# Expert probabilities turned in 32x32 blocks on VectorE and placed by DMA, with the attention product in the second slot

## The chip, the cores and the metric

The kernel runs on one core of a Trainium2 chip. The metric is the device time of one execution in microseconds. Beside the times stands one profiled execution of the same program; every row quoted below is from its trace. TensorE (PE) multiplies matrices and writes PSUM banks, VectorE (DVE), ScalarE (ACT) and GpSimd (POOL) work elementwise, SyncE (SP) issues the DMAs.

## What is computed

The input x is (8, 512, 256). It is normalized, and two branches are added to it: a causal attention with 16 heads of width 16, and a block whose attention is a mixture of experts, followed by two layer norms and a feed-forward net. Nearly all time goes into the expert attention and the causal one, which the kernel does together, a pair of heads of one batch at a time:

```python
def _gate(x, Wsel):
    s = jax.nn.sigmoid(jnp.einsum('bsd,hed->bhse', x, Wsel))
    _, idx = jax.lax.top_k(s, K)
    mask = jax.nn.one_hot(idx, E, dtype=s.dtype).sum(-2)
    return s * mask
...
q = _rope(jnp.einsum('bsd,hdp->bhsp', x, Wq))
k = _rope(jnp.einsum('bsd,hdp->bhsp', x, Wk))
gv = _gate(x, Wsel_v)
v = jnp.einsum('bsd,bhse,hedp->bhsp', x, gv, Wv)
att = jax.nn.softmax(jnp.einsum('bhsp,bhtp->bhst', q, k) / np.sqrt(P), axis=-1)
o = jnp.einsum('bhst,bhtp->bhsp', att, v)
go = _gate(x, Wsel_o)
return jnp.einsum('bhsp,bhse,hepd->bsd', o, go, Wo)
...
score = jnp.einsum('bhqd,bhkd->bhqk', Q, K) / jnp.sqrt(jnp.asarray(D_K, x.dtype))
```

## The kernel before

There are 64 pairs: 8 batches times 8 pairs of heads. A pair is worked off in a software pipeline over two passes of a loop body. The body of step `it` does the scores and probabilities of pair `it`; beside them it does the tail of the pair before (the jobs "behind") and the preparation of the next pair (the jobs "ahead"). Only the first pass and the last ones (FIRST, LAST, TAIL) leave jobs out; 62 passes (INNER) are alike, and a step below is one of them.

A step has 8 slots. Slot s begins with the scores of unit s+1 (the last with unit 0 of the next pair). Even units are the expert attention: for one block of 128 queries, 128x512 scores for each of the two heads. Odd units are the causal attention, 128 to 512 columns wide. Behind the scores of a unit, VectorE takes the negative row maxima (`row_max`, "the maxima", L1136), ScalarE the exponentials into `probs` (`exps`, L957), and then TensorE transposes the 128x128 blocks of `probs` into PSUM (`turn(s)`, L718; 8 of them for the two heads of an even unit, 2 to 8 for an odd one), and ScalarE copies them to `pt_e` (even) or `pt_c` (odd) (`turned`, L977). That is the key-by-query form that the attention product needs.

Between these, each engine fills its slot with jobs from a table written out by hand (PE_FILL, ACT_FILL, DVE_FILL, POOL_FILL). Each engine runs its own list strictly in order and waits on semaphores for the others. The jobs are:

- P 0 to 3 (PE, L673): projections of the next pair for a block of 128 rows; ScalarE copies the result to `raw`.
- CH 0 and CH 1 (DVE, L1181 to L1205): the two halves of the choice of the two best experts, from `raw`.
- V 0 to 7 (PE, L673): the values of all experts; VectorE multiplies with the gates and sums over the experts (L1157, L1159), the gate of V 0 after CH 1.
- QK 0, 1 (PE, L745), QH (ACT), QL (DVE): the queries and keys turned, in two parts of high and low order. RP, RS, RA, PC on GpSimd, PA, PB, SQ, SK on ScalarE, ST on PE and SO on ScalarE prepare rotation and the causal operands.
- AT (PE, L773): the attention product of the pair before, 16 matmuls of 512 columns from `pt_e` and `v_sb`. VC (POOL, L569) copies the next values to `v_sb` once AT is done.
- ON (DVE, L1232): AT's bank times `scale` to `oo`, which frees the bank. U e (DVE, L1239): `oo` times the output gate of expert e, to `uf`. UH e (ACT, L1041) and UL e (POOL, L573): high and low part of it.
- J e (PE, L799): six matmuls of `u_h`, `u_l` with the output weights of expert e, into two banks of sums. YA (DVE, L1245) adds the sums to `y_sb` at the end of the step.
- AC (PE, L785), its eviction (ACT) and VA: the causal product.

P, V, QK, AT and AC take two PSUM banks in turn, in the order of PE_FILL, and wait until the bank's last content has been taken. In both tables V 0 takes the bank that AT had, so it waits for ON.

SP's list in a step is: two stores of the causal output, two loads of `go` (the output gates, spread over the partitions), a load of `xx` when V 3 is done, four small stores of the reciprocal sums, two loads of them as `scale`, a load of `xx` when V 7 is done, two loads of `go`, four stores of the gates. Once in 8 steps it also loads new weights.

## Time and profile before

| | us |
|---|---|
| median of 3 runs | 3404.29 |
| lowest and highest | 3403.39 and 3406.31 |
| span of the profiled execution | 3401.4 |
| PE busy in it | 3233.1 (95%) |
| DVE busy | 2439.7 (72%) |
| ACT busy | 1961.5 (58%) |
| POOL busy | 1441.9 (42%) |
| DMA, share of 16 engines | 32.9% |

The profiled execution's own time is its span; the median is 2.9 us above it. How to read it: busy time is the sum over instructions; matmuls overlap at their ends, so the distance from one start to the next is the better measure of what a group costs. Rows of the view in order of time merge equal neighbours ("x8"), so the time of such a row covers all of them. "[4.37 <-ACT raw]" means that the engine had been idle for 4.37 us and what ended that. The span has a head of about 112 us before the loop, the loop, and a feed-forward tail from about 3110 us on.

### The profile page before, as it was taken

How to read it: one execution, taken by the hardware profiler on the slowest of the kernel's cores; microseconds unless marked ns; L12 is line 12 of the kernel's file. 1: busy time of each engine (PE TensorE's matmuls, PEld its weight loads, DVE VectorE, ACT ScalarE, POOL GpSimd, SP SyncE). 2: the span in 40 equal slices, each digit the busy share in tenths (PEclk: the TensorE clock that was granted, in tenths of full speed). 3: DMA queues.
4: the chain of work that ended last, by engine and by line, in shares of the span. 5: the costliest groups of instructions: out<-in, count | busy, mean ns of one | idle time of the engine just before them, and what ended most of it. 6: DMA issues, size and time to landing. Idle time of an engine off the chain costs nothing.

```text
span 3401.4 us, 64468 instructions
## 1 busy us (share of the span) xinstructions
PE 3233.1 (95%) x18240; PEld 2378.9 (70%) x18240; DVE 2439.7 (72%) x4708; ACT 1961.5 (58%) x4509; POOL 1441.9 (42%) x1215
## 2 busy tenths in 40 slices
PE   1699999999999999999999999999999999997998
PEld 1577777777777777777777777777777777775765
DVE  6577777777777777777777777777777777775554
ACT  2466666656666666666666666666666666664121
POOL 4144355445443454345543554434534543442212
PEclk9999999999999999999999999999999999999999
DMA  5223333334233333233233332333332433333221
GB/s 165 76 71 87 95 90 85 77 76 109 76 84 87 84 98 81 75 100 96 69 87 76 96 98 77 76 104 81 84 87 68 114 81 75 84 75 110 72 83 62
DMA packets 115937, 295.18 MB, mean 87 GB/s; under 512 B 33856, under 2 KB 54592, under 8 KB 99264
## 3 DMA queue, kind: packets, MB, share of 16 engines
q1 hardware_dynamic: 115904, 294.78, 32.9%
q8 instruction: 15, 0.25, 0.0%
q14 instruction: 18, 0.15, 0.0%
HBM read 262.74 MB, written 31.98 MB: 87 GB/s over the span
## 4 chain that ended last, share of the span: by engine, by line
PE 85%; issue 6%; DVE 5%; ACT 3%; DMA 1%; POOL 0%; ACTq 0%; SPq 0%; DVEq 0%; POOLq 0%
PE bank L673 27%; PE bank L799 22%; PE bank L718 9%; PE bank L773 7%; PE bank L688 5%; PE bank L905 4%; PE bank L897 3%; PE bank L693 3%; PE bank L745 2%; PE bank L754 2%; ACT probs L957 2%; DVE uf L1239 1%; DVE oo L1232 1%; PE bank L694 1%; ACT pt_e L977 1%
## 5 line engine op out<-in xcount | busy, mean ns | idle before, releaser
L573 POOL TENSOR_TENSOR u_l<-uf,u_h 128x512 fp32r<-128x512 f32 x512 | 716.1, 1409 | 722.6 <-ACT u_h L1041 722.4
L1136 DVE TENSOR_REDUCE nmax<-bank 128x1 f32<-128x512 f32 (+3 forms) x1024 | 551.8, 579 | 305.0 <-PE bank L688 297.8
L673 PE MATMUL bank<-wv_h,xx 128*128 128x512 f32 x2048 | 755.0, 410 | 7.1 <-DVE vm L1157 7.1
L957 ACT ACTIVATE probs<-bank,nmax 128x512 f32<-128x512 f32 (+3 forms) x1024 | 590.7, 610 | 253.2 <-DVE nmax L1136 253.1
L1041 ACT ACTIVATE u_h<-uf 128x512 fp32r<-128x512 f32 x512 | 321.7, 632 | 696.9 <-DVE uf L1239 683.6
L673 PEld LDWEIGHTS bank<-wv_h,xx 128*128 128x128 f32 x2048 | 386.0, 188 | 155.8 <-issue 59.6
L718 PEld LDWEIGHTS bank<-ident_sb,probs 128*128 128x128 f32 x3328 | 388.3, 141 | 106.4 <-issue 51.3
L718 PE MATMUL bank<-ident_sb,probs 128*128 128x128 f32 x3328 | 451.3, 274 | 1.6 <-ACT stackT L1032 0.9
L569 POOL TENSOR_TENSOR v_sb<-v_next,zero_hb 128x512 f32<-128x512 f32 x64 | 74.2, 1160 | 891.9 <-PE bank L773 877.4
L799 PE MATMUL bank<-u_h,wo_h 128*128 128x512 f32 x1024 | 427.1, 417 | 5.0 <-ACT u_h L1041 3.2
L1239 DVE TENSOR_TENSOR uf<-oo,go 128x512 f32<-128x512 f32 x512 | 416.2, 823 | 8.8 <-POOL u_l L573 6.6
L799 PE MATMUL bank<-u_h,wo_l 128*128 128x512 f32 x1024 | 405.9, 396 | 0.0
L799 PE MATMUL bank<-u_l,wo_h 128*128 128x512 f32 x1024 | 405.0, 396 | 0.0
L673 PE MATMUL bank<-wv_l,xx 128*128 128x512 f32 x1024 | 404.8, 395 | 0.0
L1157 DVE TENSOR_TENSOR vm<-bank,gv 128x512 f32<-128x512 f32 x512 | 348.4, 681 | 41.6 <-PE bank L673 41.5
L1159 DVE TENSOR_REDUCE v_next<-vm 128x64 f32<-128x512 f32 x512 | 351.3, 686 | 17.6
L673 PE MATMUL bank<-wq_h,xx 128*128 128x384 f32 x1024 | 280.4, 344 | 12.8 <-DMA xx<-xs_d 12.7
L977 ACT ACTIVATE pt_e<-bank 128x512 f32<-128x512 f32 x512 | 276.1, 594 | 5.1 <-PE bank L718 0.5
L799 PEld LDWEIGHTS bank<-u_h,wo_h 128*128 128x128 f32 x1024 | 192.4, 188 | 66.5 <-issue 24.4
L773 PE MATMUL bank<-pt_e,v_sb 128*64 128x512 f32 x1024 | 233.8, 598 | 0.0
L1191 DVE TENSOR_SCALAR vm<-raw 128x128 f32<-128x128 f32 x64 | 14.5, 227 | 296.6 <-ACT raw L992 296.6
L799 PEld LDWEIGHTS bank<-u_h,wo_l 128*128 128x128 f32 x1024 | 192.5, 188 | 46.5
(141 smaller groups left out, 5164.2 us busy)
## 6 DMA issues: line engine op xcount, KB each, us to landing
go<-go_d SPq DMA_DIRECT2D x256, 512.0 KB, 6.5
xx<-xs_d SPq DMA_DIRECT2D x128, 512.0 KB, 3.5
oo<-scale_d SPq DMA_DIRECT2D x128, 128.0 KB, 2.9
a_d<-a_out SPq DMA_DIRECT2D x128, 128.0 KB, 2.3
pt_c<-in_x SPq DMA_DIRECT2D x16, 512.0 KB, 4.7
st<-in_wv SPq DMA_DIRECT2D x16, 512.0 KB, 5.8
st<-in_wo SPq DMA_DIRECT2D x16, 512.0 KB, 7.2
go_d<-go_turned SPq DMA_DIRECT2D x256, 8.0 KB
```

The lines of the kernel that those rows point to most:

```text
L573: nc.gpsimd.tensor_tensor(u_l[:, e % 2], uf[:, e % 2], u_h.bitcast(f32)[:, e % 2], ALU.subtract).then_inc(ul_done, 1)
L673: last = nc.tensor.matmul(out, lhs, rhs, start=n == 1, stop=n == 3 * len(chunks))
L718: mm = nc.tensor.transpose(o[:, c * NP:(c + 1) * NP], probs[:, s % 2, j, c * NP:(c + 1) * NP], ident_sb[:])
L773: mm = nc.tensor.matmul(o[j * P:(j + 1) * P, :], v_sb[:, k, j, :], pt_e[:, j, k, :], start=k == 0, stop=k == TT - 1)
L799: mm = nc.tensor.matmul(ybank[i][:], w[:, e, c], u[:, e % 2], start=e == 0 and k == 0, stop=e == E - 1 and k == 2, skip_group_check=True)
L957: nc.scalar.activation(probs[:, s % 2, j, 0:w], sbank[j][:, 0:w], ACT.Exp, bias=nmax[:, 2 * s + j:2 * s + j + 1], **kw).then_inc(exp_done, 1)
L977: nc.scalar.activation(dst[:, j, 0:m, qt * NP:(qt + 1) * NP], tbank[j][:, 0:m * NP].rearrange("q (c m) -> q c m", m=NP), ACT.Copy).then_in ...
L1041: nc.scalar.activation(u_h[:, i % 2], uf[:, i % 2], ACT.Copy).then_inc(uh_done, 1)
L1136: nc.vector.tensor_reduce(nmax[:, 2 * s + j:2 * s + j + 1], sbank[j][:, 0:w], AX.X, ALU.max, negate=True).then_inc(nmax_ready, 1)
L1157: nc.vector.tensor_tensor(m, o[:].rearrange("q (c e) -> q c e", e=E), g, ALU.mult).then_inc(free, 1)
L1159: nc.vector.tensor_reduce(v_next[:, t, j, :], m, AX.X, ALU.add).then_inc(v_ready, 1)
L1239: nc.vector.tensor_tensor(uf[:, i % 2], oo[:, 0], go[:, i], ALU.mult).then_inc(u_ready, 1)
```

## The change

The transposes of the even units leave TensorE. VectorE gets four jobs XT 0 to 3: one instruction each that transposes `probs` of an even unit in blocks of 32x32 to a new buffer `pt_b`, which holds two units. When two are there, SP issues 16 DMAs (`spread_blocks`) that carry the blocks to their places in `pt_e`, each for one of four groups of 32 source partitions and one of four of target partitions. ScalarE no longer evicts the even turns, and its exponentials of an even unit wait until the one before has been transposed. XT 2 waits until the first 16 DMAs have landed, XT 0 of the next step and AT until the second 16 have. The queries lie in `pt_e` in another order, which ON undoes.

AT moves from slot 0 to slot 1, with AC behind it, ON and U 0 move from slot 0 to slot 1 behind CH 1, and the tables are dealt anew. The weights of the projections are staged in the buffer of the value weights, and are split by GpSimd in the third slot and not the seventh, once in 8 steps. The zeros that GpSimd adds are now read from one column.

```diff
-PE_FILL = [[("P", 0), ("P", 1), ("P", 2), ("P", 3), ("AT", 0)],
-           [("AC", 0), ("V", 0)],
-           [("J", 0), ("V", 1), ("J", 1)],
-           [("V", 2), ("J", 2), ("J", 3)],
-           [("V", 3), ("J", 4), ("V", 4)],
-           [("QK", 0), ("J", 5), ("QK", 1)],
+PE_FILL = [[("P", 0), ("P", 1), ("P", 2), ("P", 3)],
+           [("AT", 0), ("AC", 0)],
+           [("V", 0), ("J", 0), ("V", 1)],
+           [("J", 1), ("V", 2), ("J", 2)],
+           [("V", 3), ("J", 3), ("V", 4)],
+           [("QK", 0), ("J", 4), ("QK", 1), ("J", 5)],
            [("V", 5), ("J", 6), ("V", 6)],
            [("V", 7), ("ST", 0), ("ST", 1), ("J", 7)]]
-ACT_FILL = [[("P", 0), ("P", 1), ("P", 2), ("P", 3), ("EX", 0), ("UH", 0), ("UH", 1)],
-            [("AC", 0), ("VA", 0), ("PA", 0)],
-            [("UH", 2), ("UH", 3), ("VN", 0)],
-            [("UH", 4), ("UH", 5)],
-            [("UH", 6), ("PB", 0)],
-            [("QH", 0), ("QH", 1), ("UH", 7)],
-            [("SQ", 0), ("SK", 0)],
+ACT_FILL = [[("P", 0), ("P", 1), ("P", 2), ("P", 3), ("EX", 0), ("PA", 0)],
+            [("AC", 0), ("VA", 0), ("UH", 0)],
+            [("UH", 1), ("VN", 0), ("UH", 2)],
+            [("UH", 3)],
+            [("UH", 4), ("PB", 0), ("UH", 5)],
+            [("QH", 0), ("QH", 1), ("UH", 6)],
+            [("SQ", 0), ("SK", 0), ("UH", 7)],
             [("SO", 0), ("SO", 1)]]
-DVE_FILL = [[("CH", 0), ("ON", 0), ("U", 0), ("U", 1)],
-            [("CH", 1)],
-            [("U", 2), ("V", 0), ("U", 3)],
-            [("V", 1), ("U", 4), ("V", 2), ("U", 5)],
-            [("V", 3), ("U", 6)],
-            [("V", 4), ("QL", 0), ("QL", 1), ("U", 7)],
-            [("V", 5), ("RECIP", 0)],
+DVE_FILL = [[("XT", 0), ("CH", 0)],
+            [("CH", 1), ("ON", 0), ("U", 0)],
+            [("XT", 1), ("U", 1), ("V", 0), ("U", 2), ("V", 1)],
+            [("U", 3), ("V", 2)],
+            [("XT", 2), ("U", 4), ("V", 3), ("U", 5), ("V", 4)],
+            [("QL", 0), ("QL", 1), ("U", 6)],
+            [("RECIP", 0), ("XT", 3), ("V", 5), ("U", 7)],
             [("V", 6), ("V", 7), ("YA", 0)]]
-POOL_FILL = [[("VC", 0)],
-             [("UL", 0), ("UL", 1)],
-             [("UL", 2), ("RP", 0), ("UL", 3)],
-             [("RP", 1), ("UL", 4), ("RS", 0)],
-             [("RA", 0), ("UL", 5)],
-             [("UL", 6), ("PC", 0)],
-             [("UL", 7)],
-             []]
+POOL_FILL = [[],
+             [("VC", 0)],
+             [("UL", 0), ("RP", 0), ("UL", 1)],
+             [("UL", 2), ("RP", 1), ("RS", 0)],
+             [("UL", 3), ("RA", 0), ("UL", 4)],
+             [("UL", 5), ("PC", 0)],
+             [("UL", 6)],
+             [("UL", 7)]]
...
+        pt_b = sb("pt_b", [NP, 2, 4 * TT, 2, 32])
+        wq_st = st[:, 0, 0:KC * NPROJ]
...
+            def spread_blocks(it, kind, half, blocks):
+                if blocks[0] == 0:
+                    sp.wait_ge(blocks_ready, it * TT + 2 * half + 2)
+                for i in blocks:
+                    a, c = i // 4, i % 4
+                    sp.dma_start(pt_e[c * 32:(c + 1) * 32].rearrange("q j k (a s) -> q (j k) a s", a=4)[:, :, a, half * 64:(half + 1) * 64],
+                                 pt_b[a * 32:(a + 1) * 32].rearrange("q j (k c) t m -> q (j k) c (t m)", c=4)[:, :, c, :]).then_inc(pt_in[half], 16)
             def body(p, b, kind, before=None, after=None, weights=False, more=False):
                 it = p * B + b
                 if weights:
-                    sp.wait_ge(wq_split, p + 1)
+                    sp.wait_ge(wo_split[0], p + 1)
                     load_wq(p + 1)
-                    for j in range(2):
-                        sp.wait_ge(wo_split[j], p + 1)
-                        load_wv(p + 1, j)
+                    sp.wait_ge(wo_split[1], p + 1)
+                    load_wv(p + 1, 1)
                 if before is not None:
                     store_a(*before, kind, it)
+                spread_blocks(it, kind, 0, range(16))
+                if before is not None:
                     sp.wait_ge(u_ready, it * E - E // 2)
                 load_go(it, 0)
                 if more:
                     for j in range(2):
                         sp.wait_ge(wv_split[j], p + 2)
                         load_wo(p + 1, j)
+                if weights:
+                    sp.wait_ge(wq_split, p + 2)
                 if after is not None:
                     v_full(kind, it, 3)
                     load_x(after[1], 0)
+                if weights:
+                    load_wv(p + 1, 0)
                 spread_rden(it)
+                spread_blocks(it, kind, 1, range(6))
                 load_scale(it)
                 if after is not None:
                     v_full(kind, it, 7)
                     load_x(after[1], 1)
+                spread_blocks(it, kind, 1, range(6, 16))
                 if before is not None:
                     sp.wait_ge(u_ready, it * E)
                 load_go(it, 1)
...
-                    if wv_next and s == SLOTS - 2:
+                    if wv_next and s == 2:
...
-                    turned_before(6)
+                    for half in range(2):
+                        pe.wait_ge(pt_in[half], 256 * of + 256)
...
+                if s % 2 == 0:
+                    act.wait_ge(blocks_ready, n * TT + qt)
...
+                    elif name == "XT":
+                        dve.wait_ge(exp_done, it * UNITS + 4 * i + 2)
+                        if i == 2:
+                            dve.wait_ge(pt_in[0], 256 * it + 256)
+                        elif i == 0 and kind != FIRST:
+                            dve.wait_ge(pt_in[1], 256 * it)
...
-                        nc.vector.tensor_tensor(oo[:, 0], o[:], scale, ALU.mult).then_inc(free, 1)
+                        turned_q = o[:].rearrange("q (a t m) -> q t a m", a=4, t=TT)
+                        nc.vector.tensor_tensor(oo[:, 0].rearrange("q (t a m) -> q t a m", a=4, t=TT), turned_q,
+                                                scale.rearrange("q (t a m) -> q t a m", a=4, t=TT), ALU.mult).then_inc(free, 1)
```

In VectorE's list, at the start of the loop (nmax is the maxima; vm, best, gv, go_turned the choice; oo is ON, uf is U). Before:

```order
L1136 TENSOR_REDUCE nmax<-bank 128x1
...
L1191 TENSOR_SCALAR vm<-raw 128x128
...
L1232 TENSOR_TENSOR oo<-bank,oo 128x512
L1239 TENSOR_TENSOR uf<-oo,go 128x512 x2
L1136 TENSOR_REDUCE nmax<-bank 128x1
...
L1181 TENSOR_REDUCE best<-vm 128x16
...
L1205 STREAM_TRANSPOSE go_turned<-go_rows 128x64
```

And after:

```order
L1161 TENSOR_REDUCE nmax<-bank 128x1
...
L1245 STREAM_TRANSPOSE pt_b<-probs 128x32x32
...
L1216 TENSOR_SCALAR vm<-raw 128x128
...
L1161 TENSOR_REDUCE nmax<-bank 128x1
...
L1230 STREAM_TRANSPOSE go_turned<-go_rows 128x64
...
L1265 TENSOR_TENSOR oo<-bank,oo 128x512
...
L1273 TENSOR_TENSOR uf<-oo,go 128x512
```

A transpose stands ahead of the choice, and ON with the first U has moved from between its halves to behind the second.

In TensorE's list, from the last projection of the next pair on, with the semaphores waited for (pt_e is AT, pt_c is AC, wv_h is V 0, the first u_h is J 0). Before:

```order
L673 MATMUL bank<-wq_h,xx 128x384
...
L773 MATMUL bank<-pt_e,v_sb 64x512 [waits t_free1,t_free0]
L773 MATMUL bank<-pt_e,v_sb 64x512 x7
...
L718 MATMUL bank<-ident_sb,probs 128x128 x3
...
L688 MATMUL bank<-k_h,q_h 128x512 [waits exp_done]
...
L785 MATMUL bank<-pt_c,va 32x512 [waits t_free0,t_free1,va_ready,w_free1]
...
L673 MATMUL bank<-wv_h,xx 128x512 [waits wv_split0,w_free0]
```

And after:

```order
L694 MATMUL bank<-wq_h,xx 128x384
L709 MATMUL bank<-k_h,q_h 128x512 [waits exp_done]
...
L795 MATMUL bank<-pt_e,v_sb 64x512 [waits pt_in1,pt_in0]
L795 MATMUL bank<-pt_e,v_sb 64x512 x7
...
L807 MATMUL bank<-pt_c,va 32x512 [waits t_free1,t_free0]
...
L714 MATMUL bank<-stackT 128x256 [waits exp_done]
...
L694 MATMUL bank<-wv_h,xx 128x512 [waits wv_split0,w_free0]
```

AT now stands behind the even scores, waits for the DMAs instead of ScalarE's evictions, and the turn between AT and those scores is gone.

SP's list after, from the stores of the causal output to the last load of `go`:

```order
L393 DMA a_d<-a_out 64x512
...
L416 DMA pt_e<-pt_b 32x8x64 [waits blocks_ready]
L416 DMA pt_e<-pt_b 32x8x64 x15
...
L386 DMA go<-go_d 64x2048
...
L373 DMA xx<-xs_d 128x1024
...
L402 DMA scale_d<-rden_t 8x32 x3
...
L416 DMA pt_e<-pt_b 32x8x64 x5
L408 DMA oo<-scale_d 64x512 [waits rden_stored]
...
L416 DMA pt_e<-pt_b 32x8x64 x10
```

The three groups of `pt_e<-pt_b`, 16, 6 and 10, are new; the rest stands in the order of before.

## Rows read from the trace of the kernel before

**Rows 1.** One stretch: busy us of PE, PEld, DVE, ACT, POOL; clock, DMA share, GB/s.

```profile
700.00:1166.00 466.00, 459.81 (x2680) 339.95 (x2679) 347.65 (x650) 293.55 (x680) 207.76 (x181) 1.00 0.35 88
```

**Rows 2.** In order of time, PE, one step: start, us, engine, line, what, count.

```profile
1519.66 0.23 PE L693 MATMUL bank<-stackT 96*128 96x128 bf16 x1
...
1524.40 3.65 PE L773 MATMUL bank<-pt_e,v_sb 128*64 128x512 f32 x16
...
1529.00 0.50 PE L688 MATMUL bank<-k_h,q_h 64*128 64x512 f32 x2
...
1529.90 1.28 PE L785 MATMUL bank<-pt_c,va 128*32 128x512 f32 x16
...
1533.90 0.49 PE L799 MATMUL bank<-u_h,wo_h 128*128 128x512 f32 x1
...
1549.65 1.04 PE L718 MATMUL bank<-ident_sb,probs 128*128 128x128 f32 x8
1550.62 0.50 PE L688 MATMUL bank<-k_h,q_h 64*128 64x512 f32 x2
...
1554.70 0.38 PE L693 MATMUL bank<-stackT 96*128 96x512 bf16 x1
...
1566.25 0.23 PE L693 MATMUL bank<-stackT 96*128 96x128 bf16 x1
```

**Rows 3.** In order of time, DVE, the same step.

```profile
1525.10 0.23 DVE L1191 TENSOR_SCALAR vm<-raw 128x128 f32<-128x128 f32 x1 [4.37 <-ACT raw L992]
...
1528.21 0.69 DVE L1232 TENSOR_TENSOR oo<-bank,oo 128x512 f32<-128x512 f32 x1 [0.58 <-PE bank L773]
...
1531.97 1.39 DVE L1182 TENSOR_TENSOR vm<-vm,best 128x128 f32<-128x128 f32 x1
1533.40 0.29 DVE L1183 TENSOR_TENSOR vm<-vm,rank_sb 128x128 f32<-128x128 f32 x1
...
1536.46 0.72 DVE L1136 TENSOR_REDUCE nmax<-bank 128x1 f32<-128x256 f32 x2
1537.11 0.67 DVE L1239 TENSOR_TENSOR uf<-oo,go 128x512 f32<-128x512 f32 x1
...
1538.41 0.69 DVE L1159 TENSOR_REDUCE v_next<-vm 128x64 f32<-128x512 f32 x1
...
1551.62 1.29 DVE L1136 TENSOR_REDUCE nmax<-bank 128x1 f32<-128x512 f32 x2 [2.38 <-PE bank L688]
...
1555.51 0.68 DVE L1239 TENSOR_TENSOR uf<-oo,go 128x512 f32<-128x512 f32 x1
```

**Rows 4.** In order of time, POOL, the same step.

```profile
1528.23 1.16 POOL L569 TENSOR_TENSOR v_sb<-v_next,zero_hb 128x512 f32<-128x512 f32 x1 [16.62 <-PE bank L773]
1530.68 2.53 POOL L573 TENSOR_TENSOR u_l<-uf,u_h 128x512 fp32r<-128x512 f32 x2 [1.29 <-ACT u_h L1041]
1538.52 1.28 POOL L573 TENSOR_TENSOR u_l<-uf,u_h 128x512 fp32r<-128x512 f32 x1 [5.30 <-ACT u_h L1041]
```

**Rows 5.** Transposes on DVE, by tile: count, duration ns least, median, most.

```profile
L1205 DVE STREAM_TRANSPOSE go_turned<-go_rows x64: 245/245/247, 111.8 to 3027.9; 128x64 f32<-128x64 f32 x64
...
L1228 DVE STREAM_TRANSPOSE rden_t<-rden x64: 211/211/214, 160.0 to 3084.0; 128x32 f32<-128x32 f32 x64
```

**Rows 6.** Issues on SP in order of time; last, the page's row of a landing.

```profile
29.01 0.50 SPq L358 DMA_DIRECT2D xs_d<-u_l  x1
...
1559.19 1.31 SPq L397 DMA_DIRECT2D scale_d<-rden_t  x4
...
1565.09 3.36 SPq L374 DMA_DIRECT2D go_d<-go_turned  x4
...
a_d<-a_out SPq DMA_DIRECT2D x128, 128.0 KB, 2.3
```

**Rows 7.** PE ahead of the loop: a wait, and the stretch behind it.

```profile
140.34 0.28 PE L693 MATMUL bank<-stackT 96*128 96x256 bf16 x1 [3.25 <-ACT probs L957]
...
141.60:145.00 3.40, 3.40 (x15) 2.72 (x15) 3.23 (x9) 1.19 (x4) 0.00 (x0) 0.60 0.00 0
```

More of the change, by code:

```diff
@@ L112, in t_jobs @@
                 out.append(j)
-        if kind in (FIRST, INNER, LAST):
+        if kind in (FIRST, INNER, LAST) and s % 2 == 1:
             out.append(("turn", s))
@@ L347, in _ @@
             load_wq(0)
-            for j in range(2):
-                load_wv(0, j)
+            load_wv(0, 1)
             for b in range(B):
@@ L359, in _ @@
                                      part_x[b % 2][k].bitcast(f32).rearrange("q (h c) -> q h c", h=2)).then_inc(xs_out[b % 2], 16)
+                if b == 0:
+                    sp.wait_ge(wq_split, 1)
+                    load_wv(0, 0)
                 if b == 1:
@@ L408, in body @@
                 if weights:
-                    sp.wait_ge(wq_split, p + 1)
+                    sp.wait_ge(wo_split[0], p + 1)
                     load_wq(p + 1)
-                    for j in range(2):
-                        sp.wait_ge(wo_split[j], p + 1)
-                        load_wv(p + 1, j)
+                    sp.wait_ge(wo_split[1], p + 1)
+                    load_wv(p + 1, 1)
                 if before is not None:
                     store_a(*before, kind, it)
+                spread_blocks(it, kind, 0, range(16))
+                if before is not None:
                     sp.wait_ge(u_ready, it * E - E // 2)
@@ L568, in do @@
                         pool.wait_ge(v_ready, it * 8 + 8)
-                        nc.gpsimd.tensor_tensor(v_sb[:].rearrange("q t j c -> q (t j c)"), v_next[:].rearrange("q t j c -> q (t j c)"), zero_hb[:], ALU.add).then_inc(vc_ready, 1)
+                        nc.gpsimd.tensor_tensor(v_sb[:].rearrange("q t j c -> q (t j c)"), v_next[:].rearrange("q t j c -> q (t j c)"), zero_hb[:].to_broadcast([NP, S]), ALU.add).then_inc(vc_ready, 1)
                     elif name == "UL":
@@ L716, in turn @@
                         pe.wait_ge(exp_done, it * UNITS + 2 * s + j + 1)
-                        for c in range(TT if s % 2 == 0 else s // 2 + 1):
-                            mm = nc.tensor.transpose(o[:, c * NP:(c + 1) * NP], probs[:, s % 2, j, c * NP:(c + 1) * NP], ident_sb[:])
+                        for c in range(s // 2 + 1):
+                            mm = nc.tensor.transpose(o[:, c * NP:(c + 1) * NP], probs[:, 1, j, c * NP:(c + 1) * NP], ident_sb[:])
                         mm.then_inc(t_full[j], 1)
@@ L756, in turn_stack, with causal_turned @@
                     mm.then_inc(t_full[i], 1)
-                def turned_before(s):
+                def causal_turned():
                     for i in range(2):
                         if kind == TAIL:
-                            pe.wait_ge(t_free[i], t_at(LAST, it, i, ("turn", s)) + 1)
+                            pe.wait_ge(t_free[i], t_at(LAST, it, i, ("turn", 7)) + 1)
                         else:
-                            pe.wait_ge(t_free[i], t_at(INNER, it, i, ("turn", s)) + 1 - NT[i])
+                            pe.wait_ge(t_free[i], t_at(INNER, it, i, ("turn", 7)) + 1 - NT[i])
                 def attend():
@@ L852, in body @@
                         do(job)
-                    turn(s)
+                    if s % 2 == 1:
+                        turn(s)
             body(PRO, 0)
@@ L1055, in body @@
                         do(job)
-                    turned(s)
+                    if s % 2 == 1:
+                        turned(s)
             body(PRO, 0)
@@ L1213, in do @@
                         choose(i)
+                    elif name == "XT":
[4 more added lines that the diff above has]
+                            dve.wait_ge(pt_in[1], 256 * it)
+                        nc.vector.transpose(pt_b[:, :, :, i % 2, :].rearrange("q j c m -> q (j c) m"), probs[:, 0].rearrange("q j s -> q (j s)")).then_inc(blocks_ready, 1)
                     elif name == "QL":
```

18 lines of the change are left out of this document (9 added, 9 removed).

## The prediction

> **What bounds the kernel now.** I read the busy shares by stretch first. In ten steady steps of 46.6 us each TensorE is busy for 459.8 of 466.0 us, VectorE for 347.7, ScalarE for 293.6, GpSimd for 207.8, and the DMA engines for 0.35 of the time [rows 1]. So TensorE is the bound, but no other engine is far enough away to be forgotten: VectorE has 11.8 us to spare in a step. Then I read one step in order of time, from 1519.66 to 1566.25, 46.59 us [rows 2]; times below are counted from its start. The reader is to see how tightly two loops close. TensorE projects the next pair (P 0 to 3, until 4.74), runs the attention product AT there, and starts J 0, the first output product, at 14.24. VectorE sat idle 4.37 us for the projections (CH 0 starts at 5.44), and J 0 is fed by ON, U 0, UH 0 and UL 0, which run on VectorE, ScalarE and GpSimd in turn [rows 3, 4]. In the kernel before, that feed starts at 8.55 (ON) and is ready just in time. The chain of releasers is therefore TensorE nearly everywhere, yet the slack of the feed is a fraction of a microsecond.
>
> **What is removed.** Four of eight turns of a step go, those of 8 transposes. One lasts from 1549.65 to 1550.62, 0.97 us [rows 2]; four are 3.88 us. TensorE alone would fall to 46.59 - 3.88 = 42.7 us a step. ScalarE loses the eight evictions to pt_e, which is worth nothing by itself, since it isn't the bound.
>
> **What is added on VectorE.** Four block transposes of 128x1024. Two sizes are in the trace: 211 ns for 32 columns, 245 ns for 64 [rows 5]. That is 1.06 ns a column, so 0.21 + 992 x 1.06 ns = 1.27 us each, 5.1 us a step; lower bound half of it (a wider output could do two columns at once), upper bound 2.0. VectorE goes to 34.8 + 5.1 = 39.9 us, under 42.7. The first of the four, XT 0, stands ahead of CH 0, in the idle time of 4.37 us, and costs nothing there as long as the DMA of the step before has landed by 5.44 - 1.27 = 4.2.
>
> **What is moved, and this is the main term.** AT goes from the first slot to the second, so that the DMA has time. With it go ON and U 0, and in VectorE's list they now stand behind CH 1, the second half of the choice. Work the feed of J 0 again, from the start of the step:
> CH 0 starts at 5.44 as before, since P 0 to 3 aren't moved, and ends at 7.97 (the idle time of 0.58 ahead of ON at 8.55 gives this end) [rows 3]. The maxima of scores 2 take 1.25, to 9.25. CH 1 has a first step of 0.3, then L1182, which lasted 1.39 us, and 3.06 us from L1183 to the next maxima [rows 3]. L1182 is a product of 128x128 that takes 0.3 us like its neighbours when GpSimd is idle; in the rows GpSimd ran two u_l from 1530.68 to 1533.21, and L1182 ended just behind them [rows 3, 4]. So such a VectorE operation waits for a GpSimd operation that is running. Without that wait CH 1 is 3.7 and ends at 12.95. But GpSimd's copy of v (VC, 1.16 us [rows 4]) now starts when AT has been issued, at 4.74 + 0.90 (scores 2) + 3.65 = 9.3 [rows 2], 0.1 ahead of L1182: L1182 then ends at 10.8 and CH 1 at 13.8. I take this value, and keep 12.95 as the other end. ON adds 0.7: 14.5. From the start of a U to the end of its u_l the trace shows 1537.11 to 1539.80, 2.69 us [rows 3, 4]: J 0 starts at 17.3 (16.4 without the wait of L1182).
> From J 0 on, the same work is left on TensorE as before (V 1 to 7, J 0 to 7, QK, ST, all scores): 46.59 - 14.24 = 32.35, less three of the removed turns, 29.4. The step is 17.3 + 29.4 = 46.7 us. So almost all that the transposes give back is waited away at two places, V 0 (its bank is freed by ON: TensorE arrives at 9.3 + 1.3 for AC + 0.6 for the small turn and scores 3 = 11.2, and waits until 14.5) and J 0.
>
> **A second wait, at J 6.** In slot 5 VectorE now does the gate of V 4 first, then the maxima of scores 6, QL 0 and 1, and U 6. From the maxima's start to the start of U the trace shows 1551.62 to 1555.51, 3.89 us; the gate with its reduction is about 0.63 + 0.69; U to u_l is 2.69 [rows 3, 4]. From the end of V 4 to J 6 that is 7.9 to 8.1 us. TensorE needs for it slot 5, 4.08 (1550.62 to 1554.70) and 1.4 for the J that is now there too, then scores 7 and V 5, 2.0: 7.5 [rows 2]. So 0.5 us more, bounds 0 and 1.0. I take 0.6: 47.3 us.
>
> **The DMAs.** 32 are added in a step, 16 behind XT 1 and 6 + 10 behind XT 3, all on the queue of SP, each of 256 pieces of 256 bytes. No row has such a copy from the core's memory to itself. SP's issue time by rows: 0.33 us for 8 rows (1.31 for four), 0.50 for 256 pieces of 1 KB, 0.84 for a small one with its registers (3.36 for four) [rows 6]. I take 0.54 (0.50 and the gap), since that one has the same count of pieces. SP then issues for 17.3 us more and isn't full. What is queued behind them: the loads of go, x and scale, none of which becomes late by the 8.6 us, for go (0) is read in the next step, and x (0) at its start. The tight place is the second group. Counted from J 6: u_l 6 ends at 0, so U 6 at -2.0; the maxima 1.25, RECIP 0.55 and XT 3 1.27 follow, to 1.1; SP has spread the sums by then, issues 6 (3.2), the scale (1.15, to 5.5), x behind V 7 (0.4), and 10 (5.4, to 11.3). Landing from issue is 2.3 us for a copy of 128 KB [rows 6], so 1.8 more: 13.1. XT 0 of the next step has to start by J 6 + 8.6 (what TensorE has left in the step) + 4.2 = 12.8. So XT 0, and CH 0 behind it, and with them the whole feed, are late by 0.3 us. Each 0.1 us in the issue time moves this by 1.6 us; at 0.33 the term is 0, at 0.84 it is 5 us. The step is 47.6.
>
> **The clock.** TensorE would idle for 3.3 us at V 0 in each step. In the trace a wait of 3.25 us (at 140.34) was followed by 3.4 us at a granted clock of 0.60 in the mean, part of it at 1.2 instead of 2.4 GHz [rows 7]. Most of what is slowed then (V 0) is hidden by the wait of J 0. I add 0.2 us, bounds 0 and 1.7: 47.8 us.
>
> **Sum.** (47.8 - 46.6) x 62 steps of the loop = +74 us. Seven times the weights of wq are now split in GpSimd's third slot, ahead of UL 2, where they make VectorE's products wait: 1.5 us each by the pattern of L1182, +10 (0 to 20). At the end the last DMAs have no work to hide under: ten issues and a landing, +8 (4 to 12). The profiled execution spans 3401.4 us, the median of the runs is 3404.3, so the sum on the median is 3404.3 + 92 = 3496, say 3500 us.
>
> **Two rules of the Trainium skill.** "VectorE: DVE Perf Modes", Rules for kernel authors, tells to transpose 128x128 on TensorE and to keep VectorE for 32x32; by it the change goes the wrong way, as the sum does, though for another reason (the trace has the transposes cheap on both engines). "DMA: Bandwidth & Descriptors" wants 512 bytes a piece for full rate, but its section Why small descriptors are slow (HBM only) excepts copies within the core's memory; no row here shows such a copy, and by the exception the rival on bytes below falls.
>
> **Rivals.** (1) The feed isn't what decides, and TensorE keeps the gain. Were the waits at V 0 and J 0 away, the step would be 42.7 to 43.5, and the time 3404 - 3.5 x 62 = 3190. Against it stands the order: VectorE can't begin ON ahead of CH 1. A weaker form is more likely: L1182 not held, no wait at J 6, issues short. Then 16.4 + 29.4 = 45.8, and with the head and the end 3404 - 0.8 x 62 + 15 = 3370. (2) SP decides. If an issue takes 0.65 us or more, XT 0 (and XT 2, which waits for the first group) stop VectorE: at 0.65 a step is 49.5 and the time 3600, at 0.84 52.6 and 3790. For it: three kinds of issue in the trace are above 0.5. Against it: the dearest ones carry register work in the loop, and these addresses are fixed. (3) The bytes decide. 2.1 MB a step are added; at the mean of the stretch, 88 GB/s at a share of 0.35, they fill the engines for 8.3 us, a share of about 0.53 in all. At four times that price for small pieces DMA would take 50 us a step, and the time be 3650 or more. (4) The change does nothing that can be measured: the terms cancel within 7 us.
>
> **How the numbers follow.** Forecast, slower by the feed, 3430 to 3540: 0.62. SP or bytes decide, above 3540: 0.20 (0.12 of it up to 3650). Within 0.2%, about what a measurement can tell: 0.06. Faster, mostly the weak form of rival 1: 0.12. The range 3400 to 3650 leaves out 0.11 below and 0.08 above.
>
> **What would show it.** A step of 47 to 48 us between two scores 1; TensorE idle ahead of V 0 by about 3.3 us, released by VectorE's ON; ahead of J 0 by 1 to 1.4, released by u_l; 0.5 to 1 at J 6. The block transposes at 1.27 us. SP's issue of pt_e at about 0.5, and XT 0 starting near 4 in its step. TensorE's busy share near 0.88. I am wrong if ON starts well ahead of 13.6, if XT 0 waits for microseconds, or if the granted clock is low over much of the loop.

## The result, and the profile after

The changed kernel takes 3754.17 us (median of 4 runs, 3753.78 to 3755.46), against 3404.09 for the kernel before in the same session: a ratio of 1.103, 95% interval [1.101, 1.104]. It is 350 us slower. The prediction was 3500, with a range up to 3650: the sign was right, the size was not.

First the page of after: shares of the engines, the queue's share, the chain that ended last, the row of the block transposes and the row of their transfers.

```profile
PE 3193.1 (85%) x16192; PEld 2244.8 (60%) x16192; DVE 2677.2 (71%) x4964; ACT 1720.4 (46%) x3997; POOL 1392.6 (37%) x1215
...
q1 hardware_dynamic: 672960, 429.13, 47.1%
...
SPq 32%; DVE 25%; issue 15%; PE 13%; DMA 7%; ACT 3%; POOL 2%; DVEq 1%; POOLq 0%; ACTq 0%
...
L1245 DVE STREAM_TRANSPOSE pt_b<-probs 128x1024 f32<-128x1024 f32 x256 | 315.3, 1232 | 377.0 <-DMA pt_e<-pt_b 377.0
...
pt_e<-pt_b SPq DMA_DIRECT2D x2048, 64.0 KB, 2.2
```

TensorE's share fell from 95% to 85%, and the chain runs for 32% of its length through the queue of SP, for 25% through VectorE, and for 13% only through TensorE. VectorE waited 377 us for transfers. A stretch of after, in the columns of [rows 1]: TensorE 457.4 of 522 us busy, clock 0.94, DMA share 0.50.

```profile
2000.00:2522.00 522.00, 457.41 (x2369) 322.31 (x2370) 390.87 (x702) 258.25 (x607) 203.46 (x183) 0.94 0.50 118
```

Now one step, from 2037.67 to 2089.30, 51.6 us. VectorE in order of time (cf. [rows 3]), the rows of the four XT, CH 0, the first and the last operation of CH 1, and ON:

```profile
2043.93 1.25 DVE L1245 STREAM_TRANSPOSE pt_b<-probs 128x1024 f32<-128x1024 f32 x1 [5.17 <-DMA pt_e<-pt_b]
2045.10 0.18 DVE L1216 TENSOR_SCALAR vm<-raw 128x128 f32<-128x128 f32 x1
...
2048.91 0.28 DVE L1206 TENSOR_REDUCE best<-vm 128x16 f32<-128x128 f32 x1
...
2052.67 0.69 DVE L1265 TENSOR_TENSOR oo<-bank,oo 128x512 f32<-128x512 f32 x1
...
2054.67 1.24 DVE L1245 STREAM_TRANSPOSE pt_b<-probs 128x1024 f32<-128x1024 f32 x1
...
2068.08 1.25 DVE L1245 STREAM_TRANSPOSE pt_b<-probs 128x1024 f32<-128x1024 f32 x1 [0.37 <-DMA pt_e<-pt_b]
...
2079.92 1.21 DVE L1245 STREAM_TRANSPOSE pt_b<-probs 128x1024 f32<-128x1024 f32 x1
...
2095.51 1.25 DVE L1245 STREAM_TRANSPOSE pt_b<-probs 128x1024 f32<-128x1024 f32 x1 [5.13 <-DMA pt_e<-pt_b]
```

SP's issues in the same step (cf. [rows 6]):

```profile
2055.93 10.55 SPq L416 DMA_DIRECT2D pt_e<-pt_b  x16
...
2080.03 1.31 SPq L402 DMA_DIRECT2D scale_d<-rden_t  x4
2081.45 3.96 SPq L416 DMA_DIRECT2D pt_e<-pt_b  x6
2085.45 1.25 SPq L408 DMA_DIRECT2D oo<-scale_d  x2
2086.95 0.38 SPq L373 DMA_DIRECT2D xx<-xs_d  x1
2087.38 6.57 SPq L416 DMA_DIRECT2D pt_e<-pt_b  x10
```

And TensorE (cf. [rows 2]): the wait at V 0, the first product of J 0, the wait at J 6, and the stretch of V 0 and J 0 with its clock.

```profile
2053.42 0.80 PE L694 MATMUL bank<-wv_h,xx 128*128 128x512 f32 x1 [2.97 <-DVE oo L1265]
...
2056.33 0.79 PE L821 MATMUL bank<-u_h,wo_h 128*128 128x512 f32 x1
...
2080.51 0.47 PE L821 MATMUL bank<-u_h,wo_h 128*128 128x512 f32 x1 [1.56 <-POOL u_l L594]
...
2053.42:2059.05 5.63, 5.63 (x12) 3.97 (x13) 5.13 (x8) 2.52 (x7) 4.22 (x4) 0.50 0.16 33
```

**The loop.** One buffer pt_b serves both groups, so XT 2 may start only when the first group has left it, and XT 0 of the next step only when the second has. With the issues this makes one closed chain: from the start of XT 0 to the end of XT 1 11.98 us of VectorE's list; the first group, 16 issues and a landing, 12.17; from XT 2 to the end of XT 3 13.05; the second group, with the scale and x between, 14.38. The sum is 51.58 us, the step; it has to be, since the four stretches join end to end. What shows that it is the cause is the order inside: the first transfer of each group starts within 0.4 us of the end of XT 1 or XT 3, and XT 0 waits for the last landing in every step. XT 2 is looser: its wait changes from 0 to 1.9 us from step to step, and in a fifth of the steps it comes up to 0.7 us after the landing. TensorE isn't in the chain; VectorE waits for ScalarE once, 1.5 us ahead of QL 0. Of the chain 32 x 0.66 = 21.1 us are issues.

### The profile page after: what moved, and what is told of

Same layout as the page of the kernel before. It is cut to its first block, busy times and chain, and to the rows that moved or that the text cites. A ratio compares the mean times of both kernels' runs of the same rounds, so it can differ in the third digit from the quotient of the medians.

```text
span 3752.4 us, 61780 instructions
## 1 busy us (share of the span) xinstructions
PE 3193.1 (85%) x16192; PEld 2244.8 (60%) x16192; DVE 2677.2 (71%) x4964; ACT 1720.4 (46%) x3997; POOL 1392.6 (37%) x1215
## 4 chain that ended last, share of the span: by engine, by line
SPq 32%; DVE 25%; issue 15%; PE 13%; DMA 7%; ACT 3%; POOL 2%; DVEq 1%; POOLq 0%; ACTq 0%
SPq L416 27%; DMA pt_e<-pt_b 6%; DVE nmax L1161 5%; DVE uf L1273 4%; PE bank L928 4%; PE bank L920 3%; PE bank L694 2%; PE bank L821 2%; DVE vm L1182 2%; DVE pt_b L1245 2%; SPq L408 2%; SPq L402 2%; ACT probs L982 2%; DVE vm L1225 1%; DVE oo L1265 1%
## 5 line engine op out<-in xcount | busy, mean ns | idle before, releaser
L594 POOL TENSOR_TENSOR u_l<-uf,u_h 128x512 fp32r<-128x512 f32 x512 | 690.7, 1351 | 1193.5 <-ACT u_h L1065 1190.4
L694 PE MATMUL bank<-wv_h,xx 128*128 128x512 f32 x2048 | 809.4, 438 | 191.1 <-DVE oo L1265 184.0
L694 PEld LDWEIGHTS bank<-wv_h,xx 128*128 128x128 f32 x2048 | 422.8, 206 | 332.8 <-DVE oo L1265 198.2
L821 PE MATMUL bank<-u_h,wo_h 128*128 128x512 f32 x1024 | 466.0, 455 | 163.4 <-POOL u_l L594 129.3
L1245 DVE STREAM_TRANSPOSE pt_b<-probs 128x1024 f32<-128x1024 f32 x256 | 315.3, 1232 | 377.0 <-DMA pt_e<-pt_b 377.0
L1182 DVE TENSOR_TENSOR vm<-bank,gv 128x512 f32<-128x512 f32 x512 | 347.7, 679 | 144.9 <-PE bank L694 144.9
L694 PE MATMUL bank<-wv_l,xx 128*128 128x512 f32 x1024 | 435.0, 425 | 0.0
L821 PE MATMUL bank<-u_l,wo_h 128*128 128x512 f32 x1024 | 425.3, 415 | 0.0
L1001 ACT ACTIVATE pt_c<-bank 128x128 f32<-128x128 f32 (+3 forms) x512 | 193.9, 430 | 124.8 <-PE bank L739 124.7
L694 PEld LDWEIGHTS bank<-wv_l,xx 128*128 128x128 f32 x1024 | 212.8, 208 | 39.4
L821 PEld LDWEIGHTS bank<-u_l,wo_h 128*128 128x128 f32 x1024 | 207.5, 203 | 30.8
```

What stands on the lines that cost most here:

```text
L594: nc.gpsimd.tensor_tensor(u_l[:, e % 2], uf[:, e % 2], u_h.bitcast(f32)[:, e % 2], ALU.subtract).then_inc(ul_done, 1)
L694: last = nc.tensor.matmul(out, lhs, rhs, start=n == 1, stop=n == 3 * len(chunks))
L821: mm = nc.tensor.matmul(ybank[i][:], w[:, e, c], u[:, e % 2], start=e == 0 and k == 0, stop=e == E - 1 and k == 2, skip_group_check=True)
L1182: nc.vector.tensor_tensor(m, o[:].rearrange("q (c e) -> q c e", e=E), g, ALU.mult).then_inc(free, 1)
L1245: nc.vector.transpose(pt_b[:, :, :, i % 2, :].rearrange("q j c m -> q (j c) m"), probs[:, 0].rearrange("q j s -> q (j s)")).then_inc(block ...
```

## The experiments

By "step" I mean the median distance from one ON to the next, from the starts of ON in the trace over the whole steps: 46.60 us before, 51.58 after. A "thin" kernel makes almost no transfers; its results are wrong, and only its time is of use.

**1. Almost no transfers.** `range(16)` of the first group and `range(6)` of the second become `range(1)`, `range(6, 16)` goes (and the waits are for 16 in place of 256).

> The changed kernel, but of the 16 DMAs of each group only the first is issued (2 instead of 32 in a step), so most of pt_e keeps its zeros and the expert attention is wrong. Everything else, all waits included, stays. Theory SP (the issue time of 0.66 us makes the transpose XT 0, and the choice behind it, start 2.0 us late in each step of 51.6): XT 0 no longer waits, CH 0 starts 5.4 us into the step, a step is 49.5 or less, the time 3620 at most. Theory feed (the order CH 1 ahead of ON costs TensorE most): after that TensorE still idles some 3 us ahead of V 0, and the time stays above 3404. If issue and bytes were all of it, the time would fall to about 3190.

Measured: 3612.7 us (3590.8 and 3634.6), ratio 1.060 [1.045, 1.076], step 49.0 (mean 49.5, for every other step is 50). So the transfers cost some 140 of the 350 us, and three fifths of the loss are something else. The two runs are 44 us apart, so this holds to some 20 us; the profiled execution is the faster one. VectorE no longer waits for a transfer, TensorE still waits 3.35 us at V 0:

```profile
2015.53 0.80 PE L693 MATMUL bank<-wv_h,xx 128*128 128x512 f32 x1 [3.35 <-DVE oo L1265]
```

**2 to 4. The order on VectorE, transfers kept.** CH 0 ahead of XT 0; then ON and U 0 ahead of CH 1; then both.

```diff
-DVE_FILL = [[("XT", 0), ("CH", 0)],
-            [("CH", 1), ("ON", 0), ("U", 0)],
+DVE_FILL = [[("CH", 0), ("XT", 0)],
+            [("ON", 0), ("U", 0), ("CH", 1)],
```

> The changed kernel with XT 0 behind CH 0 in VectorE's first slot and not ahead of it, nothing else. XT 0 waits for the last DMA until 6.3 us into the step; CH 0 could start at 5.4 and ends at 8.0, when the DMA has landed. Theory SP: CH 0 starts 2.0 us earlier, XT 0 then costs its 1.2 us in the feed: 0.8 us less in a step, about 3704. If the lateness of XT 0 cost nothing (theory feed alone), the time would rise by the 1.2 us that now stand in the feed, to about 3830.

> The changed kernel with ON and U 0 ahead of CH 1 in VectorE's second slot, nothing else. Theory feed: V 0 no longer waits for ON (the 3.0 us of idle go) and J 0 starts about 4 us earlier; a step falls from 51.6 to 48 (then the loop from XT 3 over SP's 16 issues to the next XT 0 closes it), the time to about 3530. Theory SP alone (the order is harmless, only XT 0's wait counts): 3754 as before, within 20 us.

> Both orders changed: CH 0 ahead of XT 0, and ON and U 0 ahead of CH 1. If both theories hold, the two waits are gone together: CH 0 starts at 5.4, V 0 doesn't wait, and a step comes near 44 to 46, the time to 3260 to 3400. If the two losses were one and the same, it is no faster than the better of the two single changes.

Measured: 3743.0, 3822.7 and 3808.4 us; steps 51.4, 52.7 and 52.6. The first gained 11 us where 50 were expected: CH 0 could start only at 2035.34, when the projections came, and by then the transfers had landed (2.2 us after the last issue, near 2034.9). So XT 0 now waited for CH 0 in place of the DMA, and the loop was only 0.2 us shorter. The two others were misses, in sign. With ON first TensorE no longer waited at V 0, but CH 1 then ran while GpSimd did u_l and the rotation, two of its operations grew by 1.2 us together, and XT 1 behind it came that much later; XT 2 waited for it in turn:

```profile
2037.12 1.06 DVE L1210 TENSOR_TENSOR vm<-vm,best 128x128 f32<-128x128 f32 x1
2038.22 0.70 DVE L1224 TENSOR_TENSOR vm<-vm 128x128 f32<-128x128 f32 x1
...
2054.81 1.25 DVE L1245 STREAM_TRANSPOSE pt_b<-probs 128x1024 f32<-128x1024 f32 x1 [1.70 <-DMA pt_e<-pt_b]
```

That is the loop once more: what is put ahead of XT 1 counts in full, what TensorE wins counts for nothing.

**5. ON first, without transfers.**

> Only the first of the 16 transfers of each group is made (the other blocks of pt_e stay zero), and ON and U 0 stand ahead of CH 1 on VectorE. Two edits that were run apart: the first alone gave 3612.7 us, the second alone, on the full changed kernel, 3822.7. Theory A (once the transfers are gone, the step of 49.6 us is set by TensorE, which waits 3.35 us at V 0 for oo, and the second edit failed only because it made the loop through the transfers longer): ON comes 3.8 us earlier, the 3.35 us go and with them most of the half clock of V 0, step 45.5 to 47, 3360 to 3450 us. Theory B (VectorE's own list sets the step, with or without the transfers; CH 1 behind ON runs against GpSimd and grows): no gain, 3590 to 3680.

Measured: 3606.3 us, ratio 1.060 [1.058, 1.062]: no gain, as theory B said. TensorE's 3.35 us at V 0 are gone, and reappear ahead of the J, held by u_l (264 us in all, 106 in run 1).

**6. Two queues.** 14 of the 32 transfers are issued by ScalarE (`nc.scalar.dma_start`), 18 by SP.

> A complete kernel. Of the 32 block transfers of a step 14 are issued from ScalarE's queue (4 behind UH 1, 4 behind UH 2, 3 behind UH 7, 3 behind SO 1) and 18 from SP (8, 5 and 5); same bytes, same pieces. Theory A (the time it takes one queue to issue, 0.66 us each, sets the step): the two passes of the loop lose 8 and 6 issues, 9.2 us, of which the step can give back only 2.0 us before it meets the 49.6 us of the kernel with one transfer a group: 3600 to 3670 us. Theory B (the bytes or the pieces set it, at the DMA engines): 3740 to 3770. Theory C (ScalarE is held 0.66 us by each issue, 9.2 us a step, and the high and low parts of U come later): above 3770.

Measured: 3682.4 us, ratio 1.083 [1.081, 1.085], step 50.7. The DMA engines move the same bytes in less time (share 0.54 in place of 0.50), and the kernel is 72 us faster. So the queue's time was the limit, not the bytes. The time lies 12 us above the range of theory A, and far from B and C. XT 2 waits no more; XT 0 still does (4.5 us in the mean), as its group has issues behind SO 1 and behind x.

**7. One issue's price, two ways.** First other shapes in the thin kernel, then two small transfers more at the head of each group of the full one.

> Six transfers in each group in place of 16: two of 32 partitions x 8 pieces x 256 bytes (64 KB, as in the changed kernel), one with 4 pieces a partition, one with 1 piece, one of 16 partitions x 8 pieces, one of 32 partitions x 8 pieces x 64 bytes. The rest of pt_e stays zero. It asks what sets the 0.66 us between two issues on SP. Theory A (the number of pieces): 0.66, 0.33 with half the pieces or half the partitions, 0.1 with 32 pieces, and 0.66 with short pieces. Theory B (bytes): 0.66, 0.33, 0.1, 0.33, 0.17. Theory C (a fixed price per transfer): 0.6 for all.

```profile
2031.60 0.66 SPq L417 DMA_DIRECT2D pt_e<-pt_b  x1
2032.30 0.65 SPq L419 DMA_DIRECT2D pt_e<-pt_b  x1
2032.99 0.61 SPq L421 DMA_DIRECT2D pt_e<-pt_b  x1
2033.64 0.60 SPq L423 DMA_DIRECT2D pt_e<-pt_b  x1
2034.28 0.61 SPq L425 DMA_DIRECT2D pt_e<-pt_b  x1
2034.94 0.60 SPq L427 DMA_DIRECT2D pt_e<-pt_b  x1
```

In this order: 64 KB twice, half the pieces a partition, one piece a partition, half the partitions, short pieces. From start to start it is 0.70 us for 256 pieces and 0.64 for 32 pieces. Theory C held: it is a price per transfer, hardly one of pieces, and not one of bytes. (One run, 3649.8 us; only its rows are used.)

> The changed kernel as it is, with two more transfers at the head of each group, of 8 KB each, from a constant tile to a place nobody reads; 36 transfers a step on SP in place of 32. Theory A (both groups lie in one closed loop with VectorE, and each costs the issue price of 0.66 us): 4 x 0.66 = 2.6 us a step, 164 us, 3900 to 3930. Theory B (only one group is waited for, as the prediction had it): 1.3 us a step, 3825 to 3845. Theory C (bytes, not issues): 3750 to 3765.

```profile
2007.59 0.79 SPq L416 DMA_DIRECT2D more_d<-ident_sb  x2
2008.42 10.57 SPq L419 DMA_DIRECT2D pt_e<-pt_b  x16
...
2033.88 0.77 SPq L416 DMA_DIRECT2D more_d<-ident_sb  x2
2034.70 4.03 SPq L419 DMA_DIRECT2D pt_e<-pt_b  x6
```

Measured: 3855.6 us, which is in none of the three ranges: 10 us above B, 44 below A. These issues were cheaper than expected, 0.83 and 0.82 us a pair, 1.65 us a step; 62 steps of that are 102 us, the time rose by 101.4, and the step by 1.63 (53.21). Had only one group been waited for, it would have been 51. So with the price that the rows show, which was known only afterwards, each issue of both groups is on the path in full. The trace has it for the first group alone, too: from the end of XT 1 to the start of XT 2 it was 12.1 to 12.2 us in most steps of the changed kernel, and is 13.0 in nearly all of them here. Why these cost 0.41 and the others 0.66 stays open; the destination and the pattern differ.

**8. The clock.** In the thin kernel idle products (128 columns by 512, read by nobody) are put ahead of V 0: first 12, behind a wait for a turn's bank, then 8 into the bank of Y, without a wait.

> One transfer of 16 in each group, and 12 extra products of 128 columns by 512 ahead of V 0 in the step, whose result nobody reads; they fill the 3.35 us that TensorE waits there. Theory A (the half clock of V 0 and J 0 is what is left of the loss, and it comes from this gap): V 0 and J 0 take 2.8 us less, the execution's time at half clock falls from 368 us to below 60, 3420 to 3480 us. Theory B (the half clock lies beside work that VectorE has to do anyway): the clock rises and the time stays, 3580 to 3640. If the extra products themselves last past the wait, they add up to 2.6 us a step, and the time rises.

> As the kernel with 12 idle products, but 8 of them, and into TensorE's bank for Y, which is free then, so that they wait for nothing: they last 3.35 us at half clock, as long as the wait of 3.35 us that they fill, and V 0 should start when it did. Theory A (half clock at V 0 and J 0 is on the path): those two take 2.8 us less, step 46.8, 3410 to 3470. Theory B (U 1 on VectorE, behind CH 1 and XT 1, is what J 1 waits for, so a faster J 0 only waits longer): 3560 to 3640.

Measured: 3851.0 and 3556.6 us. The first says little: the wait for the bank lasted 4.9 us and the products 5.0, so V 0 was 6.6 us late; yet the step grew by 4.6 only. In the second the eight products took 2.1 us at full clock, not the 3.35 expected, and V 0 still waited 1.45. But V 0 and J 0 did run at 2.4 GHz (clock of the stretch 2000 to 2520: 1.00 in place of 0.94), and the step fell only from 49.0 to 48.6, in the mean from 49.5 to 48.9. So the half clock costs some 0.5 us a step by the two traces, and up to 0.9 by the medians of the runs (56 us). The rest of what it gives back is waited away: ahead of J 0 1.26 us, for which the trace names no releaser, and ahead of later J for u_l. That is the way of theory B, 3 us below its range.

**9. Without the transposes.** In the thin kernel each XT is cut from 1024 to 32 columns.

> The kernel with one transfer of 16 in each group (3612.7 us, step 49.6 us), and each of VectorE's four transposes cut from 1024 columns to 32: 1.23 us becomes about 0.2, and 4.1 us of VectorE's work leave a step. The rest of the turned tile stays zero. Theory A (what is left of the loss is the time that the transposes hold VectorE, ahead of the U and V products that TensorE waits for): step 45.5 us, 3330 to 3400 us. Theory B (the moved AT and ON, and the wait of TensorE at V 0 with its half clock, are what is left): at most one transpose (XT 0, ahead of CH 0) counts, 3510 to 3590. The transposes cost nothing at all: 3600.

Measured: 3598.0 us, ratio 1.057 [1.055, 1.059], against 3606 and 3613 for its neighbours. In this order the 4.1 us of VectorE's transposes cost nothing that these runs can tell (0.3 us a step). That leaves the order, which the next run tests.

**10. The order from before, without transfers.** All four tables as before the change; XT behind U 1, ahead of U 2, ahead of V 3 and behind RECIP.

```diff
 PE_FILL = [[("P", 0), ("P", 1), ("P", 2), ("P", 3), ("AT", 0)],
...
+DVE_FILL = [[("CH", 0), ("ON", 0), ("U", 0), ("U", 1), ("XT", 0)],
+            [("CH", 1)],
+            [("XT", 1), ("U", 2), ("V", 0), ("U", 3)],
```

> One transfer of 16 in each group, and all four tables as they were before the change (AT at the end of slot 0, ON, U 0 and U 1 in slot 0), with XT 0 behind U 1, XT 1 ahead of U 2, XT 2 ahead of V 3 and XT 3 behind RECIP; TensorE's turns of the even slots stay away. Theory A (the move of AT to the second slot is what costs, the 3.9 us of TensorE's turns are won and VectorE had room for its 5.0): step 43.5 to 46 us, 3220 to 3390. Theory B (the 5.0 us of VectorE cost the same in any order): 3480 to 3620. In between: VectorE's time is paid in part and the move in part.

Measured: 3395.0 us (3391.1 to 3397.1), ratio 0.9967 [0.9955, 0.998], step 45.9. So the new order costs some 200 us where transfers don't hide it: AT's move and all that was dealt anew with it, for the run took back all four tables at once and doesn't part them. The time is 5 us above the range of theory A. But the turns that TensorE lost, put at 3.88 us a step, bought only 0.7. Its two new waits, in a step that began near 1990:

```profile
1998.98 0.28 PE L713 MATMUL bank<-stackT 96*128 96x256 bf16 x1 [1.73 <-ACT probs L981]
...
2009.36 0.47 PE L820 MATMUL bank<-u_h,wo_h 128*128 128x512 f32 x1 [1.42 <-POOL u_l L593]
```

TensorE was busy for 46.0 us of a step before (459.8 of 466, [rows 1]) and is for 42.8 here, so 3.2 us less and not 3.88. With 1.73 and 1.42 that is 45.9, the step. The waits of before were 0.6, so they grew by 2.5. A stretch of this run, in the columns of [rows 1]:

```profile
700.00:1166.00 466.00, 430.46 (x2374) 305.43 (x2374) 390.62 (x696) 255.04 (x603) 201.91 (x180) 1.00 0.35 90
```

Besides, in every eighth step J 4 waits 2.8 us; the trace names no releaser, and in its list it waits there for new weights of wo to be split. Those steps take 48.9 to 50.5 where the same ones before took 46.5 to 46.9, some 30 us in all. Without them the gain of this run would be nearer 1% than 0.3%:

```profile
1549.89 0.47 PE L820 MATMUL bank<-u_h,wo_h 128*128 128x512 f32 x1 [2.79 <-issue]
```

**11. The same without the transposes.**

> As the kernel with one transfer of 16 and the order from before the change (3395.0 us, step 45.8 us), with VectorE's four transposes cut to 32 columns each (4.1 us of VectorE's less a step). The order from before with TensorE's 3.9 us of turns away gave only 9 us of the 240 that 62 steps of 3.9 us would be. Theory A (VectorE's transposes ate it): step 42.0 to 43.2 us, 3160 to 3250. Theory B (something else ate it: GpSimd's u_l, on which the J wait, or the exp on ScalarE): 3370 to 3400.

Measured: 3322.4 us, ratio 0.976 [0.975, 0.978], step 44.8: between the theories. The transposes cost 1.1 us a step here; the wait of 1.73 fell to 0.7, for XT 0 stands ahead of the maxima of scores 2. The 1.4 us for u_l stayed, and TensorE was busy for 42.7 us of a step, as in run 10. So of TensorE's 3.2 us VectorE's transposes took 1.1, the feed of J 3 through GpSimd about as much as its wait, 1.4, and 0.7 were won.

**12. The order from before, all transfers kept.**

> A complete kernel: the changed kernel with all 32 transfers, and the four tables as before the change (AT in slot 0), XT placed as in the thin kernel of that order. It undoes the move of AT and leaves the transfers. By the loop: XT 0 to the end of XT 1 7.9 us, the first group 12.2, XT 2 to the end of XT 3 11.8, the second group 14.3 until AT may start, from AT to XT 0 5.8: 52.0 us a step in place of 45.8, 3750 to 3790 us. Rival (AT and the first group waited for at different times, so that the delays overlap): 3590 to 3700.

Measured: 3747.5 us (3747.2 to 3750.2), step 51.2; 3 us below the range by the loop, far from the rival's. Within 7 us of the changed kernel. So the two costs don't add: while the loop of transfers stands, the order is worth nothing, and 3395 or 3600 below it can't be seen.

**13. Two attempts to keep the gain, both complete.** Through device memory: each group out with one transfer of 1 MB and back with four, 10 issues in place of 32. And two queues in the order from before, 23 issues on SP and 9 on ScalarE, x ahead of the scale.

> A complete kernel. All four tables as before the change, with the four XT placed as in the run before; pt_b lies in the order (c, jk, s), each group goes out to device memory with one transfer of 1 MB and comes back with four of 256 KB in pieces of 2 KB: 10 issues a step in place of 32, and XT 2 and XT 0 wait only for the transfer out. Theory A (the number of issues was the cost of the transfers, and the order the rest): 0 to 60 us above the run with thin transfers in the same order, 3240 to 3400, faster than both kernels if below 3395. Theory B (out and back takes longer than the 8 us from XT 3 to AT): TensorE waits at AT, 62 us for each us of a step, 3420 to 3600. Theory C (bytes and packets at the DMA engines were the cost): 3650 or more, since 4 MB are moved in place of 2.

> A complete kernel, the best that these runs point to: the order from before the change, 23 of 32 transfers on SP (10; then 4, the x load, 4, the scale load, 5) and 9 on ScalarE's queue (3 behind UH 2, 3 behind UH 3, 3 behind SO 1). By the issue price of 0.66 us and a landing of 2.3 us the first group is in when XT 2 comes, the second 1.3 us after AT could start; the three issues behind SO 1 hold ScalarE's copies for P by up to 1.3 us: step 47 to 48, 3460 to 3530 us. Rival (the order leaves no slack anywhere, every issue on ScalarE counts): 3600 to 3700. It beats the kernel before only if nothing of this is on the path: 3395.

Measured: 3868.1 and 3512.2 us. The first missed: x is queued behind the way back, and TensorE waits for it in every step (331 us in all; DMA share 0.57). Its number is also that of theory C, the doubled bytes, and x landed 7.6 us after its issue in place of 5.6; this run doesn't part the place in the queue from the bytes.

```profile
2007.09 0.66 PE L702 MATMUL bank<-wq_h,xx 128*128 128x384 f32 x1 [4.89 <-DMA xx<-xs_d]
```

The second came where the price of an issue put it (step 47.5; expected 47 to 48): AT waits 1.6 us for the second group, the rest are the waits of the thin kernel. It is 242 us faster than the changed kernel and still 3.2% slower than the one before. No version with all its transfers beats the kernel before; the same order without them is 0.3% below it.

## Why the prediction failed, point by point

The step was put at 47.8 us and is 51.6. The 3.8 us are two terms of the sum, about half each: the DMAs, put at 0.3 us and worth 2.1 to 2.6 (51.6 less the 49.0 to 49.5 of the thin kernel), and the feed with its clock, put at 47.5 us and measured at those 49.0 to 49.5. The forecast had the feed set the step; in the runs the loop of transfers set it.

- **Removed work** was put a little high: 3.88 us a step, while TensorE's busy time fell by 3.2 (46.0 to 42.8, run 10). The 42.7 forecast for what is left meets the 42.8 by luck, for the 46.59 that it starts from hold 0.6 us of waiting.
- **The transposes**: forecast 1.27 us, measured 1.20 to 1.25. "Costs nothing there as long as the DMA has landed" was the right condition, and it wasn't met: XT 0 waited 5.17 us.
- **The DMAs: here the mechanism failed, in price and in count.** The issue was taken as 0.54 us ("since that one has the same count of pieces") and is 0.66; the count of pieces hardly matters (run 7). And "each 0.1 us in the issue time moves this by 1.6 us" counted one group. XT 2 waits for the first group as XT 0 does for the second, with hardly any slack between them, so it is 32 issues and 3.2 us; run 7 showed that dose, 102 us by the rows of the pairs, 101 measured. The rival "SP decides" named the mechanism and priced it by the same 16: it gave 49.5 us a step and 3600. Adding 32 x 0.12 = 3.8 us to the 47.8 would give 51.6, but that is luck: the 47.8 came from the feed, which was 1.5 to 2.0 us too low by itself. The rows of the loop give it without the feed: at 0.54 an issue the loop would be 51.6 - 3.8 = 47.8 us, below the thin kernel's step, and so the time still near 3600.
- **The move of AT**: ON started at 15.0 in the step, forecast 13.8 (the 14.5 of the prediction is its end). CH 0 was 2.0 us late for the transfers; L1182 (now L1207) wasn't held, since the copy of v ended at 2048.91, when CH 1 began, so CH 1 took 3.8 in place of 4.55 us. The two make the 1.2. In the thin kernel, where CH 0 isn't late, that operation is held as forecast: 1.05 us.

```profile
2047.87 1.04 POOL L590 TENSOR_TENSOR v_sb<-v_next,zero_hb 128x512 f32<-128x512 f32 x1 [14.41 <-PE bank L795]
```

```profile
2010.59 1.05 DVE L1207 TENSOR_TENSOR vm<-vm,best 128x128 f32<-128x128 f32 x1
```

- **Waits of TensorE**: at V 0 forecast 3.3, measured 2.97; at J 6 0.6 and 1.56; at J 0 1 to 1.4, and none, since V 0 at half clock lasted 2.9 us and filled it. J 0 started at 18.7, forecast 17.3. Without transfers the step is 49.0 to 49.5, so the feed alone was put 1.7 to 2.2 us too low (47.3 before DMA and clock). The half clock explains 0.5 to 0.9 of that and the waits for u_l (1.6 us a step in the thin kernel, 0.6 put at J 6) about 1.
- **The clock**: 0.2 forecast, 0.5 to 0.9 in the thin kernel. That it costs nothing while the transfers decide follows from the loop; no run shows it.
- **The bytes** (rival 3) fell: share 0.50, worked out 0.53, and run 6 moved the same bytes 72 us faster.
- Of the 350 us, 62 steps of 4.98 are 309. The other 41, for which 18 were put, lie at the two ends of the loop: the first ON comes 15.5 us later (191.3 in place of 175.8), and the last two steps, which have less work for TensorE, took 41.9 and 29.4 us before but 48.2 and 48.4 after, for the loop of transfers holds them too. The steps with weights, put at 10 us, and the stretch behind the last ON (1.6 us more) hardly count.

## What to carry to other kernels

When a change adds a buffer that is filled, emptied by transfers and filled again in one step, write the loop down from one fill to the next before anything else: each issue in it counts as often as the buffer is turned over, and no freed engine helps. Price an issue per transfer, and by more than one kind of transfer in the trace, with the dearest as a case of its own. A bound of 95% on one engine says little about what removing work from it brings: here 3.2 us a step of TensorE's time were worth 0.7 in the order from before without transfers, and 1.8 with VectorE's part left out too, since two feeds stood just behind it.
